# Spreading a layer's post-processing between one-hots, adding a bias on TensorE, and folding five nodes behind the last tile

## The reference

```
# block 1: three graph convolutions
h_list = [x]
for l in range(3):
    hw = h_list[l] @ conv_w[l].T
    agg = segment_sum(hw[src] * dinv[src] * dinv[dst], dst)     # + self loops
    h_list.append(elu(agg + conv_b[l]) + h_list[l])
x = layernorm(x + concat(h_list) @ lin_w.T + lin_b)
# block 2: a relational convolution, 8 relations as mixes of 4 bases
W = einsum('rb,bio->rio', w_comp, bases)
agg = segment_sum(x[src] * edge_weight, edge_type * N + dst)    # 8 x N rows
x = layernorm(x + sum over r of agg[r] @ W[r])
```

## Time and profile before

| | |
|---|---|
| median of 3 runs | 1109.1 us (1108.51 to 1109.41) |
| profiled execution, its own time | 1110.03 us |
| its span (first to last instruction) | 1108.2 us |
| PE matmuls busy | 1013.3 us, 91% |
| DVE busy | 802.2 us, 72% |
| ACT busy | 444.9 us, 40% |
| POOL busy | 510.5 us, 46% |
| granted TensorE clock, mean | 0.959 of full |

### The profile page before, as it was taken

One profiled execution on the slowest core, in us unless ns is written; L12 is line 12 of the kernel. 1 busy time (PEld: TensorE's weight loads), 2 busy tenths in 40 slices (PEclk: granted clock), 3 DMA queues, 4 the chain that ended last, 5 costly groups with the idle time before them and its releaser, 6 DMA issues.

```text
span 1108.2 us, 23482 instructions
## 1 busy us (share of the span) xinstructions
PE 1013.3 (91%) x9508; PEld 665.9 (60%) x9508; DVE 802.2 (72%) x1702; ACT 444.9 (40%) x1027; POOL 510.5 (46%) x542
## 2 busy tenths in 40 slices
PE   1677898889999999999399999999999999999997
PEld 1565565556644475448266666666666666666664
DVE  4689999898526764898786677777677777767753
ACT  1588898888400030004443233233233333333320
POOL 5044000000047700000377777777777777777773
PEclk9877999899999999999589999999999999999999
DMA  5263000000101010010522222222222222222221
GB/s 155 57 193 87 7 1 2 1 1 1 59 15 27 18 59 1 1 58 14 134 54 54 59 54 58 60 54 58 59 54 58 59 53 58 59 51 58 58 53 36
DMA packets 48801, 55.34 MB, mean 50 GB/s; under 512 B 15543, under 2 KB 39129, under 8 KB 48182
## 3 DMA queue, kind: packets, MB, share of 16 engines
q0 software_dynamic: 16240, 31.95, 11.5%
q1 hardware_dynamic: 32454, 21.87, 6.9%
HBM read 42.10 MB, written 8.49 MB: 46 GB/s over the span
## 4 chain that ended last, share of the span: by engine, by line
PE 68%; DVE 18%; issue 6%; SPq 2%; ACT 2%; DMA 2%; DVEq 1%; POOL 0%
PE ps L1684 21%; PE ps L1537 21%; PE ps L1663 11%; PE ps L1678 9%; DVE arena L1107 8%; SPq L681 2%; PE ps L1526 2%; DVE dinv_all L1336 2%; DVE hT L1296 1%; PE ps L1697 1%; PE ps L1691 1%; DVE u L1330 1%; PE ps L1484 1%; DMA dinv_col<-dinv_scratch 1%; DVE arena L1259 1%
## 5 line engine op out<-in xcount | busy, mean ns | idle before, releaser
L837 POOL DMA_INDIRECT arena<-x_scratch,arena x437 | 413.4, 946 | 164.6 <-issue 126.2
L1537 PE MATMUL ps<-arena,u 125*128 125x480 fp8e5 (+1 forms) x1575 | 361.3, 356 | 1.2 <-ACT arena L891 1.2
L972 ACT COPY arena<-ps 125x400 f32<-125x400 f32 x364 | 170.2, 525 | 354.6 <-PE ps L1678 325.6
L1684 PE MATMUL ps<-arena,u 125*128 125x448 f32 x650 | 297.8, 539 | 0.0
L1537 PEld LDWEIGHTS ps<-arena,u 125*128 125x128 bf16 x1575 | 153.1, 98 | 108.1 <-ACT arena L891 1.7
L1663 PE MATMUL ps<-hT,arena 128*128 128x160 f32 x874 | 200.0, 321 | 2.6 <-DVE hT L1296 2.1
L1107 DVE TENSOR_TENSOR arena<-arena 128x2048 bf16<-128x2048 bf16 (+2 forms) x158 | 188.7, 1253 | 16.5 <-PE ps L1526 13.4
L1663 PEld LDWEIGHTS ps<-hT,arena 128*128 128x128 f32 x874 | 144.1, 190 | 87.3 <-issue 74.1
L1526 PE MATMUL ps<-arena 128*128 128x125 bf16 x1256 | 150.5, 234 | 32.4 <-DVE arena L1107 30.7
L1678 PEld LDWEIGHTS ps<-dinv_all,u 64*128 64x128 bf16 x4368 | 109.1, 96 | 103.5 <-issue 82.8
L1526 PEld LDWEIGHTS ps<-arena 128*128 128x128 bf16 x1256 | 108.2, 105 | 86.0 <-DVE arena L1107 47.9
(11 more groups left out here) (187 smaller groups left out, 712.9 us busy)
## 6 DMA issues: line engine op xcount, KB each, us to landing
arena<-x_scratch,arena POOLq DMA_INDIRECT x437
arena<-hT SPq DMA_DIRECT2D x2, 1562.5 KB, 7.1
edge_scratch<-arena SPq DMA_DIRECT2D x5, 403.0 KB, 5.2
arena<-in_x_dram SPq DMA_DIRECT2D x1, 1562.5 KB
dinv_all<-dinv_scratch SPq DMA_DIRECT2D x1, 1562.5 KB, 8.3
h_scratch<-hT SPq DMA_DIRECT2D x1, 1562.5 KB, 6.1
first_term_scratch<-arena SPq DMA_DIRECT2D x1, 1562.5 KB
arena<-first_term_scratch SPq DMA_DIRECT2D x1, 1562.5 KB
```

What stands on the lines that cost most here:

```text
L837: nc.gpsimd.indirect_dma_start(out=gat[:, j, :], out_offset=None, in_=x1_d, in_offset=bass.IndirectOffsetOnAxis(ap=idxg[:, j:j + 1], axis= ...
L972: nc.scalar.copy(o, ps[0:BLK, octet_bank(k, w), 0:4 * ND].rearrange("p (i m) -> p m i", i=4)).then_inc(s_se, 1)
L1537: return T.matmul(ps[:, agg_bank(l, c), 0:CW[c]], u[0:BLK, s, k, :], region[:, s, 0:CW[c]], start=(first and s == 0 and k == 0), stop=(end ...
L1684: last = T.matmul(ps[:, 5, 0:NB * DN].rearrange("p (b n) -> p b n", b=NB), xb[0:BLK, s, :], sD[half][0:BLK].rearrange("p (b v) n -> p b v ...
```

## The change

Three edits and what they need.

1. `post` takes a list of steps. In the first layer all pairs of a chunk are now written out (no hardware loop), and `post(0, c - 2)` is taken in four steps behind pairs 2, 3, 4 and 5 (counted from 0): the scaling; the minimum; the maximum and the addition; the last addition. Its waits for the stored features move to pair 1 of chunk 2, the two operations on `wpos` to pair 7 of chunk 4, and ACT's exponential behind its block pair 2.
2. The bias is no longer added on DVE. SyncE loads it as one row, GpSimd writes a row of ones, and each of the 25 blocks of the first term gets a second matmul of one row with one row, which adds the bias in PSUM. The broadcast load goes.
3. In the last chunk two dense products follow each of the first tiles instead of one, `finish_dense` comes ahead of the last tile, and DVE adds up the five nodes before and between the statistics instead of behind them, in a tile of its own; the order of the normalisations changes with it.

```diff
             sp.wait_ge(s_idxs, 1)
+            sp.dma_start(linrow[0:1, :], lin_b.rearrange("(o d) -> o d", o=1)).then_inc(s_row, 16)
             sp.wait_ge(s_dinv, 1)
...
-            sp.dma_start(linbB[:, :], lin_b.rearrange("(o d) -> o d", o=1).broadcast_to([P, D])).then_inc(s_back[1], 16)
...
             pool.wait_ge(s_idxs, 1)
+            nc.gpsimd.memset(onesrow[0:1, :], 1.0).then_inc(s_one, 1)
...
-                if c >= 2:
-                    exps(0, c - 2)
                 for i in range(1, (GPC if c < NCH - 1 else LASTG) // 2):
                     for slot in range(2):
                         write_block(c, i, slot)
+                    if c >= 2 and i == 2:
+                        exps(0, c - 2)
...
-            def post(l, c):
+            def post(l, c, steps=range(4)):
...
             for c in range(1, NCH):
-                for pair in range(2):
-                    onehots(GPC * c + 2 * pair, pair, False)
-                if c == 2:
-                    dve.wait_ge(s_u, NUB)
-                    dve.wait_ge(s_hs, 16)
-                    dve.wait_ge(s_dinva, 16)
-                if c >= 2:
-                    post(0, c - 2)
-                if c == 4:
-                    dve.wait_ge(s_stl, 224)
-                    link(V.tensor_scalar(wposf[:, :, :], wposf[:, :, :], 0.0, float(E - NW), ALU.max, ALU.min))
-                    V.tensor_copy(wpos[:, :, :], wposf[:, :, :]).then_inc(s_wpos, 1)
-                with dve.Fori(1, (GPC if c < NCH - 1 else LASTG) // SLOTS) as i:
-                    for pair in range(2):
-                        onehots(i * SLOTS + (GPC * c + 2 * pair), pair, False)
+                for t in range((GPC if c < NCH - 1 else LASTG) // 2):
+                    onehots(GPC * c + 2 * t, t % 2, False)
+                    if c == 2 and t == 1:
+                        dve.wait_ge(s_u, NUB)
+                        dve.wait_ge(s_hs, 16)
+                        dve.wait_ge(s_dinva, 16)
+                    if c >= 2 and 2 <= t < 6:
+                        post(0, c - 2, (t - 2,))
+                    if c == 4 and t == 7:
+                        dve.wait_ge(s_stl, 224)
+                        link(V.tensor_scalar(wposf[:, :, :], wposf[:, :, :], 0.0, float(E - NW), ALU.max, ALU.min))
+                        V.tensor_copy(wpos[:, :, :], wposf[:, :, :]).then_inc(s_wpos, 1)
...
                 if c == RELS // 2 + 1:
-                    dve.wait_ge(s_back[4], 16)
-                    link(V.tensor_tensor(yt[0:BLK], yt[0:BLK], linbB[0:BLK, None, :].broadcast_to([BLK, NBLK, D]), ALU.add))
                     dve.wait_ge(s_cq, 3)
...
+            dve.wait_ge(s_back[4], 16)
             for t in range(NUB + 1):
...
                 ahead_of(C, 2)
+                link(V.tensor_tensor(few, accN[0][:, :, AT:AT + LNODES], carry[:, :, 0:LNODES], ALU.add))
                 stats_dense(DH - 1, 6)
-                stats(C - 1)
-                norm_dense(DH - 1, False)
-                few = aggf[:, :, 0:LNODES]
-                link(V.tensor_tensor(few, accN[0][:, :, AT:AT + LNODES], carry[:, :, 0:LNODES], ALU.add))
                 dve.wait_ge(s_mu, C * TB + -(-LTILES // BT))
                 V.tensor_tensor(few, accN[2][:, :, 0:LNODES], few, ALU.add).then_inc(s_af, 1)
+                norm_dense(DH - 1, False)
+                stats(C - 1, 3)
+                stats_last()
                 norm(C - 1, False)
-                stats_last()
                 norm_last()
...
                     for q, s in enumerate(blocks_of(j)):
-                        last = T.matmul(ps[0:BLK, 7, D * q:D * (q + 1)], hT[:, BLK * s:BLK * (s + 1)], linI[:, :], start=True, stop=True)
+                        last = T.matmul(ps[0:BLK, 7, D * q:D * (q + 1)], hT[:, BLK * s:BLK * (s + 1)], linI[:, :], start=True, stop=False)
+                        last = T.matmul(ps[0:BLK, 7, D * q:D * (q + 1)], onesrow[0:1, :], linrow[0:1, :], start=False, stop=True)
...
                     tile(C, j, LTILES)
-                    if j < DLEFT:
-                        dense(TPB - DJ + j, 0)
-                    if j == LTILES - 1:
+                    for k in range(2 * j, min(2 * j + 2, DLEFT)):
+                        dense(TPB - DJ + k, 0)
+                    if j == LTILES - 2:
+                        pe.wait_ge(s_dv, DH - 1)
                         finish_dense(DH - 1, 6)
-                        pe.wait_ge(s_af, C)
-                        pe.wait_ge(s_dv, DH - 1)
-                        finish(C - 1)
+                pe.wait_ge(s_af, C)
+                finish(C - 1, 3)
                 pe.wait_ge(s_af, C + 1)
                 for b in range(NB):
-                    last = T.matmul(ps[0:LNODES, 7, 0:D], aggf[:, b, 0:LNODES], basesS[:, b, :], start=(b == 0), stop=(b == NB - 1))
+                    last = T.matmul(ps[0:LNODES, 7, 0:D], few[:, b, :], basesS[:, b, :], start=(b == 0), stop=(b == NB - 1))
```

More of the change, by code:

```diff
@@ L214, in build_program @@
         h_old = [carve(at, N, fp32, 4) for at in (0, A_H1, A_H2)]
+        linrow = carve(0, D, fp32, 4)
+        onesrow = carve(512, BLK, fp32, 4)
         srcI = carve(12544, TS, u32, 4)
@@ L220, in build_program @@
         wE = carve(A_W, EC, fp32, 4)
-        linbB = carve(A_LB, D, fp32, 4)
         nodeD = carve(A_NODE, PAIRS, fp32, 4)
@@ L250, in build_program @@
         idxg = carve(A_BN + 736, TPB, u32, 4)
+        few = carve(12000, NB * LNODES, fp32, 4).rearrange("p (b n) -> p b n", b=NB)
+        assert 12000 >= 11488 + 4 * P and 12000 + 4 * NB * LNODES <= 12544
+        fstL = carve(A_BN, 16, fp32, 4)
         iota_w = carve(11264, WN, fp32, 4)
@@ L351, in build_program @@
         s_hs = sem("h_stored")
-        s_back = [sem(f"reloaded{r}") for r in range(6)]
-        s_xb = sem("x_plus_bias")
+        s_back = [sem(f"reloaded{r}") for r in range(5)]
         s_lin = sem("lin_ready")
         s_linI = sem("first_term_weights_ready")
+        s_row = sem("bias_row_loaded")
+        s_one = sem("row_of_ones_made")
         s_y0 = sem("first_term_ready")
@@ L685, in _ @@
                 sp.dma_start(raws[a][TAILR - 1:TAILR, 6, 0:LEFT], arr[E - LEFT:E].rearrange("(p e) -> p e", e=LEFT)).then_inc(s_raw[a], 16)
+            sp.wait_ge(s_idxs, 1)
+            sp.dma_start(linrow[0:1, :], lin_b.rearrange("(o d) -> o d", o=1)).then_inc(s_row, 16)
             sp.wait_ge(s_dinv, 1)
@@ L1010, in _ @@
                 act.wait_ge(s_fv, NCHK)
-                nc.scalar.activation(fst[0:LNODES, 8:9], fst[0:LNODES, 7:8], ACT.Sqrt, bias=epst[0:LNODES, 0:1]).then_inc(s_fs, 1)
+                nc.scalar.activation(fstL[0:LNODES, 8:9], fstL[0:LNODES, 7:8], ACT.Sqrt, bias=epst[0:LNODES, 0:1]).then_inc(s_fs, 1)
             with act.Else():
@@ L1144, in post @@
                 b = convb[:, ds(l, 1)]
[L1145 to L1154, removed]
+                if 0 in steps:
+                    dve.wait_ge(s_agg, NCH * l + c + 1)
+                    V.tensor_tensor(z, ps[:, agg_bank(l, c), 0:w], dinv_all[:, at:at + w], ALU.mult).then_inc(s_rd, 1)
+                    dve.wait_ge(s_rd, 2 * NCH * l + 2 * c + 1)
+                if 1 in steps:
+                    V.tensor_scalar(m, z, b, 0.0, ALU.add, ALU.min).then_inc(s_rd, 1)
+                    dve.wait_ge(s_rd, 2 * NCH * l + 2 * c + 2)
+                if 2 in steps:
+                    link(V.tensor_scalar(z, z, b, 0.0, ALU.add, ALU.max))
+                    link(V.tensor_tensor(h, h, z, ALU.add))
+                if 3 in steps:
+                    dve.wait_ge(s_exp, NCH * l + c + 1)
+                    V.scalar_tensor_tensor(h, m, -1.0, h, ALU.add, ALU.add).then_inc(s_h, 1)
+                    dve.wait_ge(s_h, NCH * l + c + 1)
             def relation(r, dense):
@@ L1221, in _ @@
             dve.wait_ge(s_hs, 32)
-            dve.wait_ge(s_back[1], 48)
+            dve.wait_ge(s_back[1], 32)
             for c in range(NCH):
@@ L1393, in stats_last @@
                     dve.wait_ge(s_fin, NCHK)
-                    yv = ystage[0:LNODES, 1, :]
+                    yv = gat[0:LNODES, 1, :]
                     link(V.tensor_tensor(yv, ps[0:LNODES, 7, 0:D], x1r[0:LNODES, NCHK - 1, :], ALU.add))
-                    link(V.bn_stats(fst[0:LNODES, 0:6], yv))
-                    V.bn_aggr(fst[0:LNODES, 6:8], fst[0:LNODES, 0:6]).then_inc(s_fv, 1)
+                    link(V.bn_stats(fstL[0:LNODES, 0:6], yv))
+                    V.bn_aggr(fstL[0:LNODES, 6:8], fstL[0:LNODES, 0:6]).then_inc(s_fv, 1)
                 def norm_last():
                     dve.wait_ge(s_fs, NCHK)
-                    link(V.reciprocal(fst[0:LNODES, 9:10], fst[0:LNODES, 8:9]))
-                    V.tensor_scalar(gat[0:LNODES, 0, :], ystage[0:LNODES, 1, :], fst[0:LNODES, 6:7], fst[0:LNODES, 9:10], ALU.subtract, ALU.mult).then_inc(s_y, 1)
+                    link(V.reciprocal(fstL[0:LNODES, 9:10], fstL[0:LNODES, 8:9]))
```

(3 more changed lines are left out.)

## The result

Before takes 1109.2 us (median of 7 runs, 1106.1 to 1111.6), the changed kernel 1101.8 us (7 runs, 1097.5 to 1105.3): ratio 0.9935, 95% interval 0.9915 to 0.9954. It is faster, by 7.4 us (0.65%) where 14.1 were forecast, and outside the range.

A forecast was written before the change was run, and what follows sets the result against it. The prediction took PE, then DVE, with their waits for each other in the first layer, as the bound. Terms 0.8 + 10.9 + 0.4 + 0 + 1.6 + 0.4 = 14.1 us off gave 1095.0 us against the median; range 1091.5 to 1100.5.

The forecast's parts named there:

- The bias on PE: Chunk 0: 25 added one-row products, counted as 0 us; bounds a gain of 1 and a loss of 3 us.
- the cover that I named: Chunk 0: PE idles and DVE is the bound, so a late build delays ACT about 1 us and the next idle absorbs it.
- signs of being wrong: First layer: stretches at clock 0.5 inside chunks 2 to 5, a longer chunk 0, or static one-hots still at 2.33 us a pair.
- The four chunks: First layer, 129.64 to 263.06 us: 133.42 us would become 122.55, 10.9 us off; bounds 4.9 and 14.1 us.
- the static pairs' pace: First layer, one-hots outside a hardware loop: 2.25 us a pair where DVE also has a post, instead of 2.33.
- the second payment: First layer: after the post's own time, each chunk pays again for PE's clock fall; the post in steps would end this.
- The fall once a chunk: Rival, first layer: PE's clock still falls at the post's third step, 1.5 us a chunk, 6 in all: 1101.0 us; chance 0.15.
- the Trainium skill's rule: First layer, PE: frequent short idles between groups of matmuls make the clock swing, so each chunk would keep a fall: 1101.0 us.
- Chunk 6: First layer: PE is the bound, only its idle can go, 0.4 of 0.7 us off.
- DVE's addition: Layer 3: the bias addition over 25 blocks, 3.49 us, leaves DVE; 1.6 us gained, PE late next; bounds 0 and 3.5.
- The tail: Last chunk: the last normalisation ends 1.9 us earlier, but SyncE's in-order stores keep only 0.4 us; bounds 0 and 1.9.
- The store of 1.25 us: End of kernel: SyncE's store L757 takes 1.25 us again and holds the last store until 1104.9 instead of 1105.27 us.

The follow-up runs named there:

- loop_unrolled: The kernel before with only DVE's loop over the one-hot pairs written out, the post whole behind the first two pairs: 1099.8 us, ratio 0.9914.
- whole_change_again: The changed kernel run once more, unchanged, in a second series: 1104.0 us, ratio 0.9945 to before.

## Why the prediction was wrong

**The step that failed** is "The bias on PE": "I count 0", with bounds from -1 to +3. The nearest row, four products in 1.04 us, was one of products of equal height; nothing in the trace before has two heights in turn. Four more products of the old pace would have added 0.9 us (4 x 0.22); measured are 3.2 - 0.9 = 2.3 us at the higher clock, since the old products lose their pace too. PE's iteration grows from 2.9 us (72.83 to 75.69 us before) to 5.0 to 6.7, above the 4.1 us of DVE's iteration before (77.37 to 81.45), and the cover that I named, that PE idles and DVE is the bound, is gone: ACT, GpSimd and DVE wait in a row. In the profiled execution chunks 0 and 1 take 3.8 us more, against a forecast of 0.8 less; that execution is the fastest, and the second profile has 14.7 us more than before (85.5 against 70.8). In the medians the price is 8.9 or 11.1 us against the same product on 128 rows. That alone puts the result outside the range: with the product on 128 rows the time is 1092.9, with no product 1094.9, both inside 1091.5 to 1100.5. Of the forecast's signs of being wrong one came: a longer chunk 0.

**The four chunks** came out as forecast in size (12.1 against 10.9) and in what shows (chunks of 30.3 us, the clock 1.00, no one-hot of chunks 2 to 5 waiting for PE). Part of the size is luck: the 133.4 us taken as the start hold four falls of the clock, and the two other profiles with before's loop have 129.2 and 129.3. The forecast's 10.9 already held the static pairs' pace, 48 x 0.08 = 3.8 us, near the 3.4 found for the loop. What it gave to the steps alone was the end of the second payment; the pairs written out by themselves end three of the four in `loop_unrolled`. I had seen the loop's 0.35 us beside the combination and not asked which part of the stall it decides. I had also written that the trace doesn't reach between idles of 0.43 and 3.99 us; it has 2.96, 3.17 and 2.97 at the next three combinations, each with a fall behind it.

**Rivals.** The fall once a chunk (0.15) would have given 1101.0, which is near what was measured; it is not what happened, as the four chunks have none. The number alone would have misled; the stage shows it. In this kernel the short idles of up to 1.10 us didn't make the clock swing, against the Trainium skill's rule that the prediction weighed (TensorE: Matmul & The Clock Gate, section A second HAM failure mode: psum-queue depth-cycling).

**Chunk 6** came out at -0.7 us where -0.4 was forecast, measured from its first one-hot.

**DVE's addition** came out at -1.5 us where -1.6 was forecast, and what was named as late next is: L1264 waits 0.64 us for PE.

```profile
501.89 0.69 DVE L1264 TENSOR_TENSOR u<-ps,arena 125x512 f32<-125x512 f32 x1 [0.64 <-PE ps L1654]
```

**The tail** gave 0.8 us instead of 0.4 in the profile (from the first L1257 to the end the kernels of the first table take 593.5 to 594.2 us with it; before and `loop_unrolled`, without it, 594.6 and 595.1), and tail alone nothing measurable. The store of 1.25 us was not repeated; SyncE's three last stores after:

```profile
1091.69 0.35 SPq L761 DMA_DIRECT2D out_dram<-arena  x1
1092.25 0.33 SPq L763 DMA_DIRECT2D out_dram<-arena  x1
1092.64 0.32 SPq L765 DMA_DIRECT2D out_dram<-arena  x1
```

## What to carry to other kernels

An added product is priced with its neighbours, not by its columns: a product of another height between full ones costs at both of its borders, and here filling its operands with zeros to 128 rows is worth 9 to 11 us. Before an engine's idle time is counted as cover, work out its whole iteration with the new work at the lower clock as well, and see whether it becomes the bound. When two parts of a change shorten the same stall, their gains don't add up, and each has to be run alone. A stage length from one execution can hold chance, such as falls of the clock that another execution doesn't have; and a landmark that the change itself moves has to be replaced by one that it doesn't. A result near a rival's number doesn't prove the rival until its stage shows it.

## What the runs showed of the hardware that was not expected

- A change of height between float32 products of 128 columns costs about 0.19 us at 2.4 GHz (0.41 against 0.22 us a product), for 64 rows as for one.
- PE busy for 14 of 14 us by the profile was still granted 1.2 GHz (98 to 112 us of whole_change_again).
- Beside an add on GpSimd of 125x3200 float32 (7.34 us) a DVE operation on two operands of SBUF took 7.28 instead of 0.66 us.
- The same idle of PE can be followed by a fall of the clock or not: of nine idles of 2.96 to 3.17 us in three kernels with the same first layer loop, five were followed by 1.2 GHz and four by 2.4 GHz.
- One chip ran the same kernel in 1308 instead of 1109 us, all of it behind the first layer; with the first layer as before, the first combination starts at 129.7 us there and at 129.6 here. The cause wasn't studied.
